# Causal attention on one core: probabilities transposed in pairs of 64-row tiles into two banks, both heads in each eviction

## What is computed

```python
def _L2_attn_ref(x, w_qkv, w_out, b_out):
    HEADS = 16; DIM_HEAD = 64; SCALE = DIM_HEAD ** (-0.5)
    ...
    sim = jnp.einsum('bhid,bhjd->bhij', q * SCALE, k)
    sim = sim + rel[None, :, :] * slopes            # -|i - j| times a slope of the head
    sim = jnp.where(causal, mask_value, sim)
    attn = jax.nn.softmax(sim, axis=-1)
    out = jnp.einsum('bhij,bhjd->bhid', attn, v)
    ...
    return out @ w_out + b_out
```

## Time and profile before

| | us |
|---|---|
| median of 3 runs | 4488.94 |
| lowest and highest run | 4485.52, 4489.14 |
| span of the profiled execution | 4486.9 |
| the attention stage within it | 987 (2387 to 3374) |

### The profile page before, as it was taken

How to read it: one execution, slowest core, us unless ns; L and a number is a source line. 1 busy time by engine, 2 the same in 40 slices (tenths; PEclk the granted TensorE clock), 3 DMA queues, 4 the chain that set the end, 5 groups by cost and what they waited for, 6 DMA issues and landing times.

```text
span 4486.9 us, 114211 instructions
## 1 busy us (share of the span) xinstructions
PE 3978.9 (89%) x46878; PEld 2213.5 (49%) x46974; DVE 3104.6 (69%) x5185; ACT 2558.3 (57%) x3768; POOL 1208.7 (27%) x1018
## 2 busy tenths in 40 slices
PE   3799999999999999767689999999997599999997
PEld 1365555555555555535454555555553233333333
DVE  7788888888888888555415665666664676767772
ACT  5456666666666666552324555555553266666665
POOL 0366656556566566210000000000000011111110
PEclk7899999999999999865578999999998699999999
DMA  0222223222222222101000000000001200000000
GB/s 18 73 64 78 68 65 80 71 74 68 64 78 73 74 69 68 45 16 24 21 17 2 4 4 4 4 4 3 2 1 61 64 19 19 19 19 19 19 1 15
DMA packets 85358, 166.79 MB, mean 37 GB/s; under 512 B 23336, under 2 KB 37336, under 8 KB 83568
## 3 DMA queue, kind: packets, MB, share of 16 engines
q1 hardware_dynamic: 84816, 159.13, 13.6%
HBM read 40.60 MB, written 8.52 MB: 11 GB/s over the span
## 4 chain that ended last, share of the span: by engine, by line
PE 48%; issue 19%; POOL 14%; DVE 11%; ACT 5%; DMA 1%; SPq 1%; POOLq 0%; DVEq 0%; ACTq 0%
POOL arena L987 7%; PE banks L1286 6%; POOL arena L991 6%; PE banks L2223 5%; PE banks L1269 4%; PE banks L1257 4%; ACT arena L2361 2%; PE banks L522 2%; PE banks L2197 2%; PE banks L2181 2%; PE banks L1305 1%; DVE arena L861 1%; DVE arena L1439 1%; PE banks L2204 1%; PE banks L2201 1%
## 5 line engine op out<-in xcount | busy, mean ns | idle before, releaser
L2435 DVE TENSOR_REDUCE arena<-banks 128x2 f32<-128x1024 f32 x512 | 614.2, 1222 | 277.5 <-PE banks L2188 141.5
L2361 ACT ACTIVATE arena<-banks 128x1024 f32<-128x1024 f32 x512 | 522.3, 1024 | 281.5 <-PE banks L2204 147.2
L987 POOL TENSOR_TENSOR arena<-arena 128x512 f32<-128x512 f32 x384 | 424.5, 1127 | 641.0 <-DVE arena L870 633.5
L991 POOL TENSOR_TENSOR arena<-arena 128x1024 f32<-128x1024 f32 x192 | 533.1, 2777 | 15.1
L1439 DVE CUSTOM_DVE_ANT_0 arena<-arena,banks 128x512 f32<-128x512 f32 (+3 forms) x640 | 361.7, 603 | 230.7 <-issue 229.2
L1382 ACT ACTIVATE arena<-banks 128x512 f32<-128x512 f32 (+3 forms) x320 | 169.9, 531 | 406.3 <-PE banks L1269 405.6
L522 PE MATMUL banks<-arena 128*128 128x512 f32 x768 | 369.0, 625 | 29.5 <-issue 13.9
L2223 PE MATMUL banks<-arena 128*32 128x256 f32 x4096 | 335.1, 394 | 12.8 <-issue 7.6
L1374 ACT ACTIVATE arena<-arena 128x128 f32<-128x128 f32 (+15 forms) x256 | 328.6, 1285 | 11.3 <-DVE arena L1451 6.3
L2536 POOL MEMSET arena<- 128x8 f32 x1 | 0.1, 110 | 1239.4 <-DVE xn L180 1239.4
L1257 PE MATMUL banks<-arena 64*128 64x512 f32 (+3 forms) x1280 | 321.4, 579 | 4.7 <-issue 3.3
(11 more groups left out here) (435 smaller groups left out, 7485.2 us busy)
## 6 DMA issues: line engine op xcount, KB each, us to landing
arena<-arena SPq DMA_DIRECT2D x768, 64.0 KB
arena<-arena SPq DMA_DIRECT2D x96, 384.0 KB, 3.6
arena<-arena SPq DMA_DIRECT2D x96, 128.0 KB, 3.4
arena<-in_lf_wqkv SPq DMA_DIRECT2D x6, 1024.0 KB, 5.4
arena<-features_k SPq DMA_DIRECT2D x32, 128.0 KB
arena<-arena SPq DMA_DIRECT2D x8, 512.0 KB
arena<-features_q SPq DMA_DIRECT2D x16, 216.0 KB
arena<-in_lf_wqkv SPq DMA_DIRECT2D x6, 512.0 KB, 3.7
```

What stands on the lines that cost most here:

```text
L987: nc.gpsimd.tensor_tensor(r[:, :, e * H2:(e + 1) * H2], q[:, j, :, (1 - e) * H2:(2 - e) * H2], s[:, j, 1, e * H2:(e + 1) * H2].unsqueeze(1 ...
L991: nc.gpsimd.tensor_tensor(a, a, lf_rb, ALU.add).then_inc(S("lf_rot" + x), 1)
L2361: nc.scalar.activation(bi_PT[n % 4], PS[:, 2 * bi_slot("S", n):2 * bi_slot("S", n) + 2].rearrange("p a b -> p (a b)"), ACT.Exp).then_inc(S ...
L2435: nc.vector.tensor_reduce(bi_max[j % 2][:, t, :, c], PS[:, 2 * slot:2 * slot + 2], AX.X, ALU.max).then_inc(S("bi_mx"), 1)
```

## The change

The transposes are done in halves. `turn` now makes of every 128 x 128 tile two transposes: the lower 64 partitions (queries 0 to 63 of the tile) go, as 128 x 64, into bank 4, and the upper 64 partitions into bank 5. Lower and upper alternate, tile after tile, head 0's tiles first and head 1's behind them in the same bank. A bank then holds, for both heads, one half of the queries. VectorE's eviction takes bank 4 with both heads and writes 64-column pieces at an offset of 0 in each 128, ScalarE's takes bank 5 and writes the pieces at an offset of 64. So `at_PT[x]` becomes one tile with a head dimension, of the same size as the two before, and `values` reads the same 256 columns out of it.

The waits move with it: both `at_ptA` and `at_ptB` are awaited ahead of the first transpose, and both `at_trA` and `at_trB` are raised by the last two transposes of the group. A semaphore that nobody waits for, `at_turning`, is raised by TensorE behind the waits.

```diff
-        at_PT = [[arena.f32_3(n, 2 * P) for _ in range(2)] for n in (NB // 2, NB)]
+        at_PT = [arena.f32(2 * n * 2 * P).rearrange("p (h k q) -> p h k q", h=2, k=n) for n in (NB // 2, NB)]
...
                 c, x, b = at_where(i)
+                n = min(4, at_row(c, x) + 1 - 4 * b)
+                if i >= 1:
+                    pe.wait_ge(S("at_ptA"), l * 80 + i)
+                    pe.wait_ge(S("at_ptB"), l * 80 + i)
                 for h in range(2):
                     if b == 0:
                         pe.wait_ge(S("at_exp"), l * 64 + (2 * (2 * c + x) + h + 1))
-                    if i >= 1:
-                        pe.wait_ge(S("at_ptB" if h else "at_ptA"), l * 80 + i)
-                    for j in range(min(4, at_row(c, x) + 1 - 4 * b)):
-                        m = nc.tensor.transpose(PS[:, 4 + h, j * P:(j + 1) * P], ck(at_E[c % 2][x][h], 4 * b + j, P), ident)
-                    m.then_inc(S("at_trB" if h else "at_trA"), 1)
+                        pe.sem_inc(S("at_turning"), 1)
+                    elif h == 0:
+                        pe.sem_inc(S("at_turning"), 1)
+                    for j in range(n):
+                        k = h * n + j
+                        lower = nc.tensor.transpose(PS[:, 4, k * at_D:(k + 1) * at_D], ck(at_E[c % 2][x][h], 4 * b + j, P)[0:at_D], ident[0:at_D, 0:at_D])
+                        upper = nc.tensor.transpose(PS[:, 5, k * at_D:(k + 1) * at_D], ck(at_E[c % 2][x][h], 4 * b + j, P)[at_D:P], ident[at_D:P, at_D:P])
+                lower.then_inc(S("at_trA"), 1)
+                upper.then_inc(S("at_trB"), 1)
...
                         m = nc.tensor.matmul(PS[h * at_D:(h + 1) * at_D, 6, x * 2 * P + o:(x + 1) * 2 * P], at_V[p][:, k, h * at_D:(h + 1) * at_D],
-                                             at_PT[x][h][:, k, o:2 * P], start=(k == 0), stop=(k == nk - 1), skip_group_check=True)
+                                             at_PT[x][:, h, k, o:2 * P], start=(k == 0), stop=(k == nk - 1), skip_group_check=True)
...
-                nc.scalar.activation(at_PT[x][1][:, 4 * b:4 * b + n, t % 2 * P:(t % 2 + 1) * P],
-                                     PS[:, 5, 0:n * P].rearrange("p (a b) -> p a b", b=P), ACT.Copy).then_inc(S("at_ptB"), 1)
+                nc.scalar.activation(at_PT[x][:, :, 4 * b:4 * b + n, t % 2 * P + at_D:(t % 2 + 1) * P],
+                                     PS[:, 5, 0:n * P].rearrange("p (h a b) -> p h a b", h=2, b=at_D), ACT.Copy).then_inc(S("at_ptB"), 1)
...
-                nc.vector.tensor_copy(at_PT[x][0][:, 4 * b:4 * b + n, t % 2 * P:(t % 2 + 1) * P],
-                                      PS[:, 4, 0:n * P].rearrange("p (a b) -> p a b", b=P)).then_inc(S("at_ptA"), 1)
+                nc.vector.tensor_copy(at_PT[x][:, :, 4 * b:4 * b + n, t % 2 * P:t % 2 * P + at_D],
+                                      PS[:, 4, 0:n * P].rearrange("p (h a b) -> p h a b", h=2, b=at_D)).then_inc(S("at_ptA"), 1)
```

## The result

| | us |
|---|---|
| change, median of 4 runs | 4437.76 (4436.75 to 4440.44) |
| before, on the same chip, median of 4 runs | 4489.04 (4485.52 to 4492.56) |
| ratio, with its 95% interval | 0.9883 (0.9869 to 0.9897) |
| span of the profiled execution | 4434.8 (before 4486.9) |

The account below looks back on a forecast made before the run. TensorE was taken to bound the stage, busy 974 of 987 us. Transposes -106, changes of shape -32 and VectorE's loss +42 gave -96 against the 4486.9 span, so 4390.9, or 4393 us as median; range 4352 to 4450.

Parts of the forecast that it names:

- Transposes: TensorE's 2176 transposes at 0.109 us become pairs of halves at 0.06: 237 us to 131, a gain of 106.
- rival 1: Loads hold a pair of half transposes at 0.11 us, so the transposes save nothing: 4476 us, chance 10%.
- Rival 2: A half-height transpose runs as an ordinary fp32 product, a pair costing 0.22 us: slower, 4699 us, chance 5%.
- Changes of shape: TensorE's switches between array shapes around transposes: gains 38 and 19, losses 22 and 3, together a gain of 32 us.
- Waits: Both evictions awaited before a group, `at_turning` put at nothing; late waking up to 0.1 us per slot, 6 us in all.
- What VectorE gives back: TensorE's saving in odd steps' slots 0 to 2 lost waiting for VectorE: 1.3 us per step, 42 us (26 to 58).
- about 0.24 of 1.58 arrives: In an odd step TensorE could save 1.58 us, but scores and logits of slot 2 come only 0.24 earlier.
- Evictions: Copies in pieces of 64 instead of 128 columns still take 0.68 us: no change taken, at most 4 us.
- Rival 3: Evictions take over everywhere, ScalarE's copy binding where VectorE's does not: another 51 us lost, 4444 us, chance 9%.
- Rival 4: Better than forecast: VectorE's loss halves as slots shift, 4370 us, chance 6%.

Follow-up runs that it names:

- Experiment 5: Changed kernel with the upper transposes also reading the lower 64 partitions, so all 4352 are in the same rows of the array: 4538.09 us, ratio 1.0089.
- Experiment 2: Kernel before, with 128-row transposes, given only the change's waits, new semaphore and VectorE copy waiting for the whole group: 4509.37 us, ratio 1.0033.
- Experiments 3 and 6: Changed kernel; 3: VectorE's eviction cut to 8 of every 64 columns, 4407.46; 6: VectorE's copy between two heads' logits, except even slots 1 and 2, 4447.37.
- experiment 12: Changed kernel with ScalarE evicting both banks in slot 4 of steps 0 and 4 and slot 1 of steps 5 and 7: 4425.82 us, ratio 0.9849.
- experiments 6 and 7: Changed kernel, VectorE's copy between two heads' logits; 6: all slots but even 1 and 2, 4447.37; 7: only even slot 4 and odd slot 1, 4452.24.
- experiment 1: Changed kernel with all lower halves of a head's tiles first and all upper halves behind them, instead of alternating: 4438.62 us, ratio 0.9871.

## Why the prediction was right, and where its gain was too high

- *Transposes, forecast -106, measured -101.* A pair costs 0.0625 us, nearly the 0.06 chosen from the earlier trace rows; that is the 5 us, over 2176 pairs. Experiment 5 shows that the gain is concurrency. The load rule of the Trainium skill (TensorE: Matmul & The Clock Gate, section LDWEIGHTS), by which a pair would have cost 107 ns, is contradicted here as it was by the earlier trace rows; that removes rival 1 (4476). Rival 2 (4699) is gone with 4352 records for 4352 transposes.
- *Changes of shape, forecast -32, measured -30,* but by errors that partly cancel: leaving 64-row transposes for a 128-row shape costs 0.20 instead of 0.15 (30 instead of 22), values ahead cost nothing extra (0 instead of 3), and the scores' side gave 40 instead of 38.
- *Waits.* I put the merged waits at nothing, `at_turning` as running ahead of the array, and the late waking at up to 0.1 us in 64 groups. Experiment 2 has all of it at 14 to 17 us in the old kernel, where VectorE could no longer start half a group early. My argument that this doesn't matter, because groups become half as long, was made for the changed kernel, and no run tests it there by itself. The waking was real and touched more groups than I had counted: 0.09 us at a held group, 0.18 at one that opens a row. With some 150 held groups my estimate from these is up to 15 us, which stand within the next term.
- *What VectorE gives back, forecast +42, measured +66:* the term that was too small. It went wrong in what it left out and not where it was worked out. In slots 0 to 2 of the odd steps the held time grew by 46 us, 1.4 us per odd step where I had 1.3. There "about 0.24 of 1.58 arrives" was still too much: from the transposes of even slot 4 to the first of the odd step's long row the four kinds of odd step took 6.98, 6.04, 9.85 and 9.44 us (medians) and take 7.15, 5.94, 9.76 and 9.22, on average 0.06 less. I had let the logits of slot 2 move up with the scores, but those scores stand behind transposes and an output product that are themselves held since slot 0. The other 19 us or so come from slots that I had put at nothing. For odd slots 3 and 4 I had set 2.5 us of TensorE against 1.8 of VectorE, and yet they lost 5 us; the even steps, which lost 11, I had not looked at.
- *Within groups and elsewhere, +9 in the stage and +3 outside it:* not in the sum. These gaps are spread over many groups, and what causes them is not shown.
- *Evictions:* unchanged at 0.68, as taken.
- *Rival 3* (4444) came close to the time and was right in that the other slots lose time too, but it is not what happened: of the 102 groups held for more than 0.12 us ScalarE's copy holds 11. Experiments 3 and 6 show that it is next as soon as VectorE is relieved. *Rival 4,* slots shifting in our favour, did not happen by itself; with the copies given out by hand (experiment 12) 11 us of the stage came back.

So the forecast's mechanism holds and its size does not: -101 - 30 + 66 + 9 + 3 = -53, against the -96 forecast and 52 between the spans. VectorE's 66 lies beyond the 58 that I allowed, so it was luck in part that the time still fell inside the range. A small slip of the sum besides: its ends, 4361 and 4449, leave out the 2.0 us between span and median that the 4393 has.

## What to carry to other kernels

Two transposes of half the height in different rows of the array took together what one of them takes alone (0.0625 and 0.065 us), so a stream of 128-row transposes can be cut nearly to half its time, and it costs a change of shape less where its neighbours have the 64-row shape already. Before counting on it, add up for each stretch, and not only for the tightest one, what the evicting engine must do between two groups: where it is level already, TensorE's saving there is worth next to nothing (0.06 us per odd step here). Then changing the order of that engine's instructions only moved the wait (experiments 6 and 7), while giving selected instructions to an engine with room at that very place paid (12).

## What the runs showed of the hardware

- The array's two row halves went through their transposes side by side, a pair every 0.0625 us, whatever the order in the program (experiment 1). In one half together, they came one every 0.065 us (experiment 5). So 64 columns of moving operand take more than half of the 0.109 us that 128 took.
- With both waits ahead of a group and the raise of a semaphore in a sequencer instruction of their own (0.05 us), TensorE started 0.15 us after the copy's end instead of 0.06 (experiment 2 and the changed kernel), and 0.23 after it where the group opens a row (2754.57 in the changed kernel).
- Out of 64-row transposes into a 128-row product the change of shape cost 0.20 us (30 us over 148 places); out of whole transposes into 64-row scores likewise 0.20, out of these scores into whole transposes 0.15.
